# Second attention of a transformer kernel: q's split stacked by DMA, reciprocals in pairs, new orders of work on every engine

## The chip, the cores and the metric

One core of a Trainium2 chip runs the whole program in one launch. The metric is the device time in microseconds (us) of one execution. Three runs of the kernel before gave 1553.55, 1548.76 and 1550.9 us, a median of 1550.9 us.

## The reference

The input is x, 1024 tokens of 256 features, in float32. Four blocks follow each other, each with a layer norm ahead of it and a residual around it:

```python
x = x + attn_a(layernorm(x), ...)   # 16 heads of 128, a window of 64 keys, low-rank additions
x = x + ffn(layernorm(x), ...)      # 16 experts (4 chosen a token) and a shared part
x = x + attn_b(layernorm(x), Wq, Wk, Wv, Wo)
x = x + ffn(layernorm(x), ...)
```

The change is in the third block, called b in the kernel:

```python
q, k, v = heads(x @ Wq, 32), heads(x @ Wk, 8), heads(x @ Wv, 8)   # heads of 64
q, k = apply_rope(q), apply_rope(k)            # t1*cos - t2*sin, t1*sin + t2*cos
k, v = repeat(k, 4), repeat(v, 4)              # 4 query heads share one key head
scores = where(causal, q @ k.T / sqrt(64), min)
out = (softmax(scores) @ v) @ Wo
```

## The kernel before, in words

Products are done to float32 accuracy from two parts of each operand: a high part (a rounded copy in the type fp32r, made by ScalarE, ACT) and a low part (value minus high part, made by VectorE, DVE). The program has five engine streams written by hand with semaphores: TensorE (PE), DVE, ACT, GpSimd (POOL) and SyncE (SP), which only issues DMAs.

**Groups, heads, tiles.** Block b goes over 8 groups (one key head each), each of 4 query heads, 32 heads in all. A head has 8 query tiles of 128 rows (`SCORE_TILES`, the order 7, 6, 5, 4, 0, 1, 2, 3); tile t has 128 (t+1) keys. Per tile: PE makes the scores (`scores`) in one of two pairs of PSUM banks; DVE takes the row maxima (`row_max_b`, L691); ACT takes the exponentials and their row sums (`exp_b`, L1096); DVE takes the reciprocal of the sum (`row_inv_b`, L698), one tile at a time; POOL multiplies (`p_norm_b`, L844). Then the probabilities are turned in 12 chunks: PE turns (`turn`, L1495) into one of two banks, ACT copies the high part (`pt_hi_b`, L1106), DVE makes the low part (`pt_lo_b`, L706), PE multiplies with v (`products`). Chunk s can be turned only when the low part of chunk s-2 is out of the bank. Two sums a head (`o_add`, L714) put the result in `ot`.

**Pieces.** While the heads of group g run, q and k of group g+1 are made in 6 pieces of 128 x 512: pieces 0 and 1 are k, 2 to 5 are q (two heads a piece, one in partitions 0 to 63, the other in 64 to 127). A piece goes: projection on PE into bank 7 (`proj`); copy by ACT (`raw_b`, L1067); times cosine by DVE (`cos_b`, L667, writes `ra`); four DMAs issued by SP that swap the halves from `raw` to `rb` (`swap`, L292); two POOL operations (`rot_b`, L829 and L833); high part by ACT (`high_b`); low part by DVE (`low_b`).

**The stack.** For the scores, the high and the low part of one q head stand one above the other in the 128 partitions of `qh`: head 0 of a pair has its high part in partitions 0 to 63 and its low part in 64 to 127, head 1 the other way round. So `high_b` writes a q piece with two copies of 64 rows (L1081, L1082) and `low_b` with two subtractions of 64 rows (L681, L683). A k piece takes one copy (L1077) and one subtraction (L677) of 128 rows.

**What sets the order.** Each engine executes its steps in the order of a table `DUE` (10000 units are one head), which `steps` sorts for each engine by itself. A step waits on semaphores, and what is behind it on its engine waits with it. `w_hi_b` and `w_lo_b` split the next group's weights. The start of the block is written out step by step (`FIRST_PIECES` gives the order of the first six pieces; `first_raw`, `first_cos`, `first_high`, `low_b`), with `head(-1, ...)` as the two partial heads before group 0.

## Time and profile before

| | before |
|---|---|
| median of 3 runs | 1550.9 us |
| the profiled execution | 1545.96 us |
| its span | 1544.1 us |
| PE busy | 1426.9 us (92%) |
| DVE busy | 1112.4 us (72%) |
| ACT busy | 856.4 us (55%) |
| POOL busy | 627.5 us (41%) |

The profile comes from one execution, 1.9 us longer than its span. "Busy" is time in which an engine executes at least one instruction; matmuls are pipelined, so that the start of one and the end of the one before overlap. Block b lies from about 620 to 1290 us of the span. A figure over the whole span is a mean of blocks with different limits, so the rows below are mostly of this block alone.

### The profile page before, as it was taken

How to read it: one execution, taken by the hardware profiler on the slowest of the kernel's cores; microseconds unless marked ns; L12 is line 12 of the kernel's file. 1: busy time of each engine (PE TensorE's matmuls, PEld its weight loads, DVE VectorE, ACT ScalarE, POOL GpSimd, SP SyncE). 2: the span in 40 equal slices, each digit the busy share in tenths (PEclk: the TensorE clock that was granted, in tenths of full speed). 3: DMA queues.
4: the chain of work that ended last, by engine and by line, in shares of the span. 5: the costliest groups of instructions: out<-in, count | busy, mean ns of one | idle time of the engine just before them, and what ended most of it. 6: DMA issues, size and time to landing. Idle time of an engine off the chain costs nothing.

```text
span 1544.1 us, 27763 instructions
## 1 busy us (share of the span) xinstructions
PE 1426.9 (92%) x8632; PEld 1197.3 (78%) x8632; DVE 1112.4 (72%) x2132; ACT 856.4 (55%) x1917; POOL 627.5 (41%) x540
## 2 busy tenths in 40 slices
PE   6999999999899999788988889789898989899998
PEld 4888888888788888667776777667777769688887
DVE  5666666657565556579999998899999977565555
ACT  1444444454343333477777777677777765433332
POOL 3555555530000001376868686668686620000000
PEclk8999999999999999999999999999999999999999
DMA  3000000001111112110101010101010001111110
GB/s 110 25 25 26 25 24 24 16 23 44 49 42 51 41 51 73 38 28 21 35 18 39 15 39 17 33 20 37 17 28 18 18 21 43 49 52 51 41 51 28
DMA packets 30138, 54.25 MB, mean 35 GB/s; under 512 B 6273, under 2 KB 13761, under 8 KB 29761
## 3 DMA queue, kind: packets, MB, share of 16 engines
q1 hardware_dynamic: 30016, 52.78, 11.7%
q8 instruction: 59, 0.97, 0.3%
q14 instruction: 63, 0.51, 0.1%
HBM read 39.13 MB, written 1.05 MB: 26 GB/s over the span
## 4 chain that ended last, share of the span: by engine, by line
PE 69%; DVE 14%; issue 9%; ACT 4%; POOL 1%; DVEq 0%; ACTq 0%; POOLq 0%
PE ps L1187 49%; PE ps L1388 8%; PE ps L1495 6%; PE ps L1333 5%; DVE pt_lo L706 3%; DVE nmb L691 2%; DVE qh L683 2%; PE ps L1275 2%; DVE qh L681 2%; ACT pt_hi L1106 1%; DVE rb L408 1%; ACT pb_low L1096 1%; DVE ot L714 1%; DVE h_lo L600 1%; DVE hf L594 1%
## 5 line engine op out<-in xcount | busy, mean ns | idle before, releaser
L706 DVE TENSOR_TENSOR pt_lo<-ps,pt_hi 128x512 fp32r<-128x512 f32 (+3 forms) x384 | 206.5, 549 | 36.3 <-ACT pt_hi L1106 34.0
L1187 PE MATMUL ps<-kh,qh 128*128 128x512 f32 (+3 forms) x768 | 194.5, 362 | 19.9 <-DVE qh L683 10.8
L1106 ACT CAST pt_hi<-ps 128x512 fp32r<-128x512 f32 (+3 forms) x384 | 176.0, 480 | 60.0 <-PE ps L1495 53.7
L691 DVE TENSOR_REDUCE nmb<-ps 128x1 f32<-128x1024 f32 (+7 forms) x256 | 191.0, 746 | 14.7 <-PE ps L1187 13.3
L1187 PEld LDWEIGHTS ps<-kh,qh 128*128 128x128 f32 x768 | 135.7, 192 | 48.8 <-ACT pb_low L1096 10.3
L1187 PE MATMUL ps<-xt_hi,wf_hi 128*128 128x512 f32 x400 | 160.7, 402 | 9.4 <-DVE wf_lo L522 9.4
L1187 PE MATMUL ps<-pt_hi,vst 128*128 128x512 f32 (+3 forms) x384 | 163.5, 426 | 0.0
L1187 PE MATMUL ps<-xt_hi,wf_lo 128*128 128x512 f32 x400 | 159.3, 398 | 0.0
L1187 PE MATMUL ps<-xt_lo,wf_hi 128*128 128x512 f32 x400 | 159.3, 398 | 0.0
L1032 ACT CAST h_hi<-hf 128x512 fp32r<-128x512 f32 x100 | 62.1, 621 | 137.8 <-DVE hf L594 137.8
L588 DVE TENSOR_TENSOR sg<-sg,cwu 128x512 f32<-128x512 f32 x88 | 62.2, 707 | 105.2 <-ACT sg L1026 105.1
L1187 PE MATMUL ps<-pt_lo,vst 128*128 128x512 f32 (+3 forms) x384 | 135.2, 352 | 0.0
L1026 ACT ACTIVATE sg<-ps 128x512 f32<-128x512 f32 x100 | 59.9, 599 | 133.2 <-PE ps L1187 133.2
L844 POOL TENSOR_TENSOR pb_odd<-pb_odd,rib 128x1024 f32<-128x1024 f32 (+1 forms) x64 | 106.7, 1674 | 51.3 <-DVE rib L698 50.7
L923 ACT ACTIVATE pa<-ps,nmax 128x192 f32<-128x192 f32 x128 | 53.1, 424 | 130.9 <-DVE nmax L442 130.9
L1388 PE MATMUL ps<-wf_hi,h_hi 128*128 128x256 f32 x400 | 113.4, 284 | 3.2 <-DVE h_lo L600 3.2
L1388 PE MATMUL ps<-wf_hi,h_lo 128*128 128x256 f32 x400 | 112.8, 282 | 0.0
L1388 PE MATMUL ps<-wf_lo,h_hi 128*128 128x256 f32 x400 | 112.7, 282 | 0.0
L799 POOL TENSOR_TENSOR pa<-pa,rinv 128x384 f32<-128x384 f32 x64 | 53.0, 828 | 134.4 <-DVE rinv L448 134.4
L1333 PE MATMUL ps<-wos,ot_hi 128*128 128x256 f32 x512 | 95.9, 289 | 3.6 <-DVE ot_lo L486 3.6
L600 DVE TENSOR_TENSOR h_lo<-hf,h_hi 128x512 fp32r<-128x512 f32 x100 | 68.9, 689 | 41.2 <-ACT h_hi L1032 39.3
L821 POOL TENSOR_TENSOR wb_lo<-wb,wb_hi 128x768 fp32r<-128x768 f32 x8 | 15.6, 1950 | 202.9 <-ACT wb_hi L1010 202.9
(169 smaller groups left out, 4082.7 us busy)
## 6 DMA issues: line engine op xcount, KB each, us to landing
wf<-in_wf SPq DMA_DIRECT2D x50, 384.0 KB, 3.0
rb<-raw SPq DMA_DIRECT2D x192, 64.0 KB, 2.0
wa<-in_wa SPq DMA_DIRECT2D x16, 384.0 KB, 3.0
wb<-in_wb SPq DMA_DIRECT2D x8, 384.0 KB, 3.0
wo<-in_wo_a SPq DMA_DIRECT2D x16, 128.0 KB, 2.0
wo<-in_wo_b SPq DMA_DIRECT2D x16, 128.0 KB, 2.0
lb<-in_lb SPq DMA_DIRECT2D x16, 72.0 KB, 3.0
x_res<-in_x SPq DMA_DIRECT2D x4, 256.0 KB, 3.6
```

The source lines that it names most:

```text
L588: v.tensor_tensor(sg[:, b, :], sg[:, b, :], cwu[:, HALF * half:HALF * half + HALF], ALU.mult).then_inc(sem(f"{s}_sgc"), 1)
L600: v.tensor_tensor(h_lo[:, b, :], hf[:, b, :], h_hi[:, b, :].bitcast(F32), ALU.subtract).then_inc(sem(f"{s}_h_lo"), 1)
L691: v.tensor_reduce(nmb[:, par, i:i + 1], ps[:, b:b + 2, :].rearrange("p b k -> p (b k)")[:, 0:P * (t + 1)], AX.X, ALU.max, negate=True).the ...
L706: v.tensor_tensor(pt_lo[:, s % 3, at], ps[:, 4 + s % 2, at], pt_hi[:, s % 3, at].bitcast(F32), ALU.subtract).then_inc(sem("b_pt_lo"), 1)
L844: g_.tensor_tensor(pb(par, t), pb(par, t), rib[:, par, i:i + 1].broadcast_to([P, P * (t + 1)]), ALU.mult).then_inc(sem("b_pn"), 1)
L1026: s_.activation(sg[:, b, :], ps[:, b, :], ACT.Silu).then_inc(sem(f"{s}_silu"), 1)
L1032: s_.copy(h_hi[:, b, :], hf[:, b, :]).then_inc(sem(f"{s}_h_hi"), 1)
L1106: s_.copy(pt_hi[:, s % 3, at], ps[:, 4 + s % 2, at]).then_inc(sem("b_pt_hi"), 1)
L1187: return t_.matmul(o, l, r, start=start, stop=stop)
L1333: ins = t_.matmul(o, (ot_hi, ot_lo)[a][:, n % OT_RING, P * m:P * m + P], wos[:, h, w, :], start=h == 0 and k == 0 and m % 2 == 0, stop=h = ...
L1388: ins = t_.matmul(o, (h_hi, h_lo)[a][:, b, P * m:P * m + P], (wf_hi, wf_lo)[w][:, slot, 2 * D:3 * D], start=first and n == 0 and m % 2 == ...
L1495: last = t_.transpose(ps[:, 4 + s % 2, P * m:P * m + P], pb(par, base + m)[:, P * block:P * block + P], idf[:, :])
```

## The change

Four edits, all in block b.

1. `high_b` of a q piece is one copy of 128 rows from `ra` to the new tile `qt_hi`, `low_b` one subtraction of 128 rows into the new tile `qt_lo`. SP then issues four DMAs of 64 rows x 2 KB a piece (`stack`) that put the quarters where `qh` wants them. `scores` waits for the DMAs of the pieces that it reads; `raw_b` waits for the DMAs of the q piece two before (same half), since `qt_hi` and `qt_lo` have one slot a half. On SP, `stack` stands behind swaps, the load of the next weights, and ahead of the swaps of later pieces.
2. `row_inv_b` runs for odd i only, on two columns.
3. The table `DUE` has new values for all steps of b; scores of tile 0 are now issued nearly a head earlier, the low part of chunks 7 to 11 and the sums `o_add` come later in DVE's order. `proj` computes the head whose `o_add` it waits for.
4. At the start, DVE and ACT do the parts of pieces 4 and 5 ahead of head(-1, 1, 3), where the first row maxima and exponentials now are; ACT's `first_raw` of pieces 3 and 5 waits for the stack DMAs of pieces 2 and 3; the split of group 1's weights comes ahead of the first head.

```diff
@@ SP
+            def stack(n, piece, r):
+                pair, at = piece // 2 - 1, slice(HALF * (piece % 2), HALF * (piece % 2) + HALF)
+                sp.wait_ge(sem("b_lo"), n + 1)
+                for part, src, dst, which in ((qt_hi, 0, 0, 0), (qt_lo, 0, 64, 0), (qt_lo, 64, 0, 1), (qt_hi, 64, 64, 1)):
+                    sp.dma_start(qh[dst:dst + 64, pair, which, at].bitcast(F32),
+                                 part[src:src + 64, r, :].bitcast(F32)).then_inc(
+                        sem(f"b_stacked{piece}"), 16)
             def group(g, gp):
-                if not (isinstance(g, int) and g >= NG - 2):
-                    load_group(g + 2)
                 if not (isinstance(g, int) and g == NG - 1):
-                    for piece in range(6):
-                        swap(6 * (g + 1) + piece, piece % 2)
+                    n = 6 * (g + 1)
+                    for piece in range(4):
+                        swap(n + piece, piece % 2)
+                    stack(n + 2, 2, 0)
+                    stack(n + 3, 3, 1)
+                    if not (isinstance(g, int) and g >= NG - 2):
+                        load_group(g + 2)
+                    swap(n + 4, 0)
+                    swap(n + 5, 1)
+                    stack(n + 4, 4, 0)
+                    stack(n + 5, 5, 1)
             load_group(1)
-            for n in range(6):
-                swap(n, n % 2)
+            swap(0, 0)
+            swap(1, 1)
+            swap(2, 0)
+            stack(1, 2, 1)
+            swap(3, 1)
+            swap(4, 0)
+            stack(3, 3, 1)
+            swap(5, 1)
+            sp.wait_ge(sem("b_vout"), NT)
+            stack(4, 4, 0)
+            stack(5, 5, 1)
@@ DVE
-                    v.tensor_tensor(qh[64:128, pair, 0, at], ra[0:64, r, :],
-                                    qh[0:64, pair, 0, at].bitcast(F32), ALU.subtract)
-                    ins = v.tensor_tensor(qh[0:64, pair, 1, at], ra[64:128, r, :],
-                                          qh[64:128, pair, 1, at].bitcast(F32), ALU.subtract)
+                    ins = v.tensor_tensor(qt_lo[:, r, :], ra[:, r, :], qt_hi[:, r, :].bitcast(F32), ALU.subtract)
-                v.reciprocal(rib[:, par, i:i + 1], rsb[:, par, i:i + 1]).then_inc(sem("b_inv"), 1)
+                v.reciprocal(rib[:, par, i - 1:i + 1], rsb[:, par, i - 1:i + 1]).then_inc(sem("b_inv"), 2)
             head(-1, 1, QPG - 2)
-            head(-1, 1, QPG - 1)
             low_b(4, 0, FIRST_PIECES[4], 0)
             low_b(5, 0, FIRST_PIECES[5], 1)
+            head(-1, 1, QPG - 1)
@@ ACT
+                if isinstance(n, int) and n < 6:
+                    if n in (3, 5):
+                        act.wait_ge(sem(f"b_stacked{FIRST_PIECES[n - 2]}"), 64)
+                else:
+                    earlier = (piece - 2) % 6
+                    if earlier >= 2:
+                        act.wait_ge(sem(f"b_stacked{earlier}"), 64 * (g + 1) if piece >= 4 else 64 * g)
-                    s_.copy(qh[0:64, pair, 0, at], ra[0:64, r, :])
-                    ins = s_.copy(qh[64:128, pair, 1, at], ra[64:128, r, :])
+                    ins = s_.copy(qt_hi[:, r, :], ra[:, r, :])
@@ PE
                     pe.wait_ge(sem("b_lo"), 6 * g + (4 if hh < 2 else 6))
+                    for piece in (2, 3) if hh < 2 else (4, 5):
+                        pe.wait_ge(sem(f"b_stacked{piece}"), 64 * (g + 1))
-                        after(pe, "b_ot", 2 * (QPG * g + hh))
+                        after(pe, "b_ot", 2 * (QPG * g + heads_before(hh, i)))
@@ DUE (three of the 17 rows)
-    "inv": [-7333, -5571, -3963, -1688, -1674, -694, 44, 2103],
+    "inv": [-3513, -3512, 158, 159, 2001, 2002, 4819, 4820],
-    "pt_lo": [673, 2143, 2647, 2921, 5181, 6125, 6452, 7556, 8136, 9242, 9746, 9869],
+    "pt_lo": [3651, 4305, 5646, 5967, 6740, 6802, 7803, 10136, 10431, 11671, 12899, 13375],
-    "low": [13396, 17882, 27446, 29557, 44833, 47488],
+    "low": [17629, 24257, 26441, 28306, 45983, 46970],
```

Per group, where k pieces are 0 and 1 and ^ marks a piece that belongs to the group before in the table, ACT's new order in the first head of a group is exp 0, chunk 3, high 4^, exp 1, chunks 4 and 5, high 5^, exp 2, chunk 6, raw 0, exp 3, chunks 7 and 8, exp 4, raw 1; DVE's is max 0, chunk 1, (reciprocal), chunk 2, max 1, chunk 3, low 4^, max 2, reciprocal, chunks 4 and 5, low 5^, max 3, chunk 6, cos 0, max 4.

## Rows read from the trace of the kernel before

**Rows 1.** The page, part 4: the chain that ended last, shares of the span.
```profile
PE 69%; DVE 14%; issue 9%; ACT 4%; POOL 1%; DVEq 0%; ACTq 0%; POOLq 0%
```
**Rows 2.** Windows: us, each engine's busy us (instructions), PEclk, DMA share, GB/s.
```profile
839.52:856.43 16.91, 15.87 (x104) 12.87 (x102) 15.99 (x36) 14.16 (x35) 13.38 (x13) 1.00 0.07 17
856.43:875.85 19.42, 15.58 (x97) 12.23 (x96) 18.64 (x37) 14.63 (x35) 12.39 (x10) 1.00 0.06 14
875.85:893.63 17.78, 17.32 (x110) 14.16 (x109) 14.55 (x32) 15.26 (x35) 12.84 (x11) 1.00 0.13 31
893.63:915.60 21.97, 18.80 (x104) 14.78 (x103) 21.38 (x38) 15.82 (x37) 17.98 (x13) 0.92 0.16 43
839.52:915.60 76.08, 67.57 (x407) 54.04 (x405) 70.57 (x139) 59.88 (x140) 56.59 (x47) 0.98 0.11 27
671.25:1235.05 563.80, 500.08 (x3005) 401.29 (x3004) 516.69 (x1013) 441.94 (x1023) 413.46 (x338) 0.97 0.10 26
```
**Rows 3.** Waits of 839.52 to 915.60: engine, line, for whom, total us, times, longest.
```profile
PE ps L1495 <- DVE pt_lo L706: 6.5, 7, 2.6
ACT pt_hi L1106 <- PE ps L1495: 6.4, 8, 2.1
DVE pt_lo L706 <- ACT pt_hi L1106: 3.6, 7, 1.9
```
**Rows 4.** Groups by line and form, DVE, 839.52 to 915.60: count, busy us, mean ns.
```profile
L683 DVE TENSOR_TENSOR qh<-ra,qh 64x512 fp32r<-64x512 f32 x4 | 6.1, 1524 | 0.1
L698 DVE RECIPROCAL rib<-rsb 128x1 f32<-128x1 f32 x33 | 4.6, 150 | 0.1
L681 DVE TENSOR_TENSOR qh<-ra,qh 64x512 fp32r<-64x512 f32 x4 | 5.4, 1358 | 0.1
L677 DVE TENSOR_TENSOR kh<-ra,kh 128x512 fp32r<-128x512 f32 x2 | 2.3, 1130 | 0.0
```
**Rows 5.** Timeline of DVE: start us, us, line, operation.
```profile
898.55 0.15 DVE L698 RECIPROCAL rib<-rsb 128x1 f32<-128x1 f32 x1
898.62 0.67 DVE L706 TENSOR_TENSOR pt_lo<-ps,pt_hi 128x512 fp32r<-128x512 f32 x1
900.26 2.18 DVE L681 TENSOR_TENSOR qh<-ra,qh 64x512 fp32r<-64x512 f32 x1
902.45 2.08 DVE L683 TENSOR_TENSOR qh<-ra,qh 64x512 fp32r<-64x512 f32 x1
904.56 0.69 DVE L706 TENSOR_TENSOR pt_lo<-ps,pt_hi 128x512 fp32r<-128x512 f32 x1
```
**Rows 6.** Timelines of POOL and PE in the same stretch; the last bracket is idle time before.
```profile
900.00 3.98 POOL L844 TENSOR_TENSOR pb_odd<-pb_odd,rib 128x1024 f32<-128x1024 f32 x2
905.30 0.44 PE L1495 MATMUL ps<-idf,z 128*128 128x128 f32 x2 [2.60 <-DVE pt_lo L706]
```
**Rows 7.** Instructions on tiles qh and raw: duration ns min/median/max, first and last start.
```profile
L1081 ACT CAST qh<-ra x32: 606/622/633, 634.7 to 1208.0; 64x512 fp32r<-64x512 f32 x32
L681 DVE TENSOR_TENSOR qh<-ra,qh x32: 684/1078/2268, 642.3 to 1212.9; 64x512 fp32r<-64x512 f32 x32
L292 SPq DMA_DIRECT2D rb<-raw x192: 507/591/781, 625.2 to 1196.3; - x192
DMA to landing us min/median/max: 1.9/2.0/3.1
```
**Rows 8.** Timelines of the block's start, 640 to 672 us: ACT, DVE, PE, POOL.
```profile
643.47 0.59 ACT L1067 COPY raw<-ps 128x512 f32<-128x512 f32 x1 [1.97 <-PE ps L1187]
642.25 0.68 DVE L681 TENSOR_TENSOR qh<-ra,qh 64x512 fp32r<-64x512 f32 x1
653.85 1.17 PE L1187 MATMUL ps<-kh,qh 128*128 128x512 f32 x4 [2.02 <-DVE qh L683]
661.63 3.54 POOL L844 TENSOR_TENSOR z<-z,rib 128x1024 f32<-128x1024 f32 x2
671.25 1.20 DVE L691 TENSOR_REDUCE nmb<-ps 128x1 f32<-128x1024 f32 x1
```

More of the change, by code:

```diff
@@ L89, in build @@
         ra = sb("ra", [P, 2, HALF])
+        own = ExitStack()
+        with own:
+            qt_hi = sb("qt_hi", [P, 2, HALF], F32R, own)
         rb = sb("rb", [P, 2, HALF])
@@ L156, in build @@
             vb = ot[:, 0, :, :].rearrange("p (g k) (t d) -> p g k t d", k=2, d=DB)[:, :, 1, :, :]
+            over = ExitStack()
+            with over:
+                qt_lo = sb("qt_lo", [P, 2, HALF], F32R, over)
             raw = sb("raw", [P, 2, HALF], c=own)
@@ L674, in low_b @@
                 r = half if r is None else r
-                at = slice(HALF * half, HALF * half + HALF)
                 if piece < 2:
+                    at = slice(HALF * half, HALF * half + HALF)
                     ins = v.tensor_tensor(kh[:, kp, 1, at], ra[:, r, :], kh[:, kp, 0, at].bitcast(F32),
@@ L722, in head @@
                         row_max_b(h, (hh + dh) % 2, i)
-                    elif kind == "inv":
+                    elif kind == "inv" and i % 2:
                         row_inv_b(h, (hh + dh) % 2, i)
@@ L1124, in head @@
                     elif kind == "raw":
-                        raw_b(piece, i)
+                        raw_b(piece, g + 1 + dh, i)
+                        if i == 5 and not (isinstance(g, int) and g + 1 + dh >= NG - 1):
+                            w_hi_b(g + 2 + dh)
                     elif kind == "high":
@@ L1130, in head @@
                             v_hi_b(g + 1, 1 - gp)
-                        if (kind, i) == ("raw", 5) and not (isinstance(g, int) and g >= NG - 2):
-                            w_hi_b(g + 2)
             def group(g, gp):
@@ L1168, in _ @@
             v_hi_b(0, 0)
+            w_hi_b(1)
             head(-1, 1, QPG - 2)
-            head(-1, 1, QPG - 1)
             first_high(4)
             first_high(5)
-            w_hi_b(1)
+            head(-1, 1, QPG - 1)
             all_groups(act, group)
@@ L1648, in pieces_before, with heads_before @@
     return 6 * g + 6 + (0 if isinstance(g, int) and g == NG - 1 else done)
+def heads_before(hh, piece):
+    return hh + (DUE["proj"][piece] % 10000 - DUE["products"][11]) // 10000 + 1
 def chunk_columns(slot):
```

35 lines of the change are left out of this document (17 added, 18 removed).

## The prediction

> **What bounds the kernel now.** I read the page first: over the span PE holds 69% of the chain that ended last and DVE 14% [rows 1]. That mean is of little use for one block, so the windows of busy time come next. Between the first row maxima of two successive groups, 839.52 and 915.60 us, lie 76.08 us; DVE is busy for 70.57 of them (93%), PE for 67.57 (89%), ACT for 59.88, POOL for 56.59 [rows 2]. In this block DVE is the fuller engine, and PE is close behind. The four heads of the group take 16.91, 19.42, 17.78 and 21.97 us, and the length follows whichever of the two is fuller: in the two long ones DVE is busy for 18.64 and 21.38 us, in the third PE is, for 17.32 of 17.78 [rows 2]. The waits say how DVE's load reaches PE: the longest entry is PE's turning of a chunk that waits for the low part, 6.5 us a group, once for 2.6 us [rows 3]. Groups by line and form say what makes the long heads long: eight subtractions of 64 rows (L681, L683), 5.4 + 6.1 = 11.5 us a group, though their fastest takes 0.684 us [rows 4, 7]. They stand one behind the other in DVE's order: at 900.26 us two of them take 2.18 and 2.08 us, the low part behind them starts at 904.56, and PE, idle for 2.60 us, goes on at 905.30 [rows 5, 6]. So the thing to price is DVE's time a group, and then how soon PE takes over as the limit.
>
> **The split of q.** Per piece two subtractions of 64 rows (1.358 + 1.524 us) become one of 128 rows. The k pieces show one of that shape, 1.130 us on average [rows 4]. Saved: 4 x (2.882 - 1.130) = 7.0 us of DVE a group. Bounds for one new subtraction: from the 0.684 us of the fastest of 64 rows to the 2.268 us of the slowest [rows 7]; that makes the saving between 11.5 - 9.1 = 2.4 and 11.5 - 2.7 = 8.8 us. I take 1.130, since it is the same shape and sits in the same traffic. On ACT one copy of 0.622 us a piece goes [rows 7], 2.5 us a group of 59.88 busy: worth nothing by itself, as ACT has 16 us of idle time a group.
>
> The spread of these subtractions has a visible cause: POOL started two multiplications of 3.98 us together at 900.00, and the two subtractions beside them end at about 902.4 and 904.5 [rows 5, 6]. The Trainium skill (SBUF — State Buffer, section "SBUF: two separate sides") says that a DVE operation with two SBUF inputs and a GpSimd operation that reads SBUF take a shared port pair as an exclusive lock for the whole instruction. The trace agrees: each of the two took about one POOL operation (3.98/2 = 1.99 us). By that rule the gain is in the number of locks asked for, four a group instead of eight, and the new table could spend it by putting all four beside POOL's longest operations; this is the second rival below, priced from the rows.
>
> **The stack DMAs.** 4 DMAs a q piece, 16 a group, on SP, beside 24 swaps and one load. An issue takes SP 0.591 us [rows 7]: 41 x 0.59 = 24 us of 76, so the queue is not full. The path matters more: low part ready, 4 issues (2.4 us), landing 2.0 us (a swap of half the bytes; bounds 1.9 to 3.1) [rows 7]: 4.4 us from the subtraction to the first user. Users are the scores two heads on, and ACT's raw copy of the q or k piece two later. By the new order low 4^ is over before max 2, and raw 0, which waits for its stack, stands behind exp 2 and chunk 6, with PE's scores, chunks and six projection matmuls before it; I count about 7 us between the two, against 0.7 + 4.4. Raw 1 and low 5^ stand alike, some 5 us apart after the landing of the other stack. Raw 4 and 5 are half a head or more behind. The swaps of raw 0 and 1 are queued on SP behind both stacks, so raw 0's land about when POOL has done its fifth multiplication and wants them, to within half a microsecond. I price all of this at 0 in steady state (at most the first user's wait, the third rival).
>
> **Reciprocals.** 16 of 32 a group go. One is 0.150 us [rows 4], but the next operation begins 0.07 us after its start (898.55, 898.62) [rows 5]: between 1.1 and 2.4 us a group, 1.1 taken. Half the tiles are released to POOL one exponential later; POOL has 19 us of idle time a group, which hides it.
>
> **The new orders.** DVE's need falls to 70.57 - 7.0 - 1.1 = 62.5 us a group. PE's stays at 67.57, less what its own short waits and lowered clock have put into it (the last head shows a granted clock of 0.92 after its stalls, the other three 1.00) [rows 2]. So PE becomes the limit, and what is late next is PE's own queue. How near it can come to being full is shown by the third head: 17.32 of 17.78, 97% [rows 2]. With 66.5 us of work and 96 to 97% the group takes about 69 us: 7.1 us less. As far as dependencies go the orders leave that room: scores, maxima and exponentials of one bank pair go round in about 10 us a head, chunks in about 9, against 17. A gain of nothing from the orders beyond the removed DVE time would give 76.08 - 8.1 = 68.0 while DVE limits, so both ways meet near 68 to 69.
> How often: from 671.25 to 1235.05 us there are 30 heads in 563.8 us [rows 2], in which all 28 of the later q pieces fall, 7 groups' worth: 7 x 7.1 = 50 us less.
>
> **The start.** Here the change costs. ACT's raw copy of piece 3, at 643.47 before, now waits for the stack of piece 2: its low part is there at about 642.3, SP is busy with a swap until 643.3, issues until 645.7 and the last lands at about 647.5: 4 us later than before. Then the swap, POOL's two operations (2 x 1.3), high and low part of piece 3, and a second stack (4.4 us): first scores at about 660 instead of 653.85 [rows 8]. Raw 5 waits for that same stack, then swap, POOL, high and low of piece 5 (0.6 + 4.4 + 2.6 + 0.6 + 0.7 = 9 us), all of it now ahead of the first maximum: about 669. From there the first head takes its old way to the first multiplications on POOL (before: 661.63) and to the next head's first maximum at 671.25 [rows 8]. I get 681 for that one, with a chunk or two more done than before: +9 us, bounds +4 (only the first wait counts) and +13.
>
> **Sum.** 1545.96 - 50 + 9 = 1505 us for an execution like the profiled one. That one lies 4.9 us below the median of the runs shown, so a median of about 1509 us.
>
> **Rivals.** (1) PE loses nearly all its waits: 65.5 us a group, if the pipelining overlaps in its 67.57 shrink too. For: PE needs no operation more. Against: two chunk banks couple three engines. 7 x 10.6 = 74 less, + 9: about 1485. (2) The lock: the four new subtractions fall beside long multiplications and take 2.27 each. DVE saves 2.4 + 1.1 = 3.5, the group 3.5 to 4: 26 less, + 9: 1534. For: max and exp order of the next head puts them right behind the first reciprocal, when POOL starts its longest pieces. Against: k's subtractions stand alike and average 1.130. (3) The stack wait on ACT's raw copies: everything behind raw 0 and raw 1, exponentials and chunks, is held until the quarters land. It decides as soon as it adds 41/7 = 5.9 us a group; two waits of the full path, 8.8 us a group, give 7 x 8.8 = 62 on top of 1509: about 1571, slower. For: raw 0 has only some 2 us to spare by my count, and SP serves in order. Against: a piece's DMAs are issued by an SP that stands waiting for them. (4) The change does what it says but the saved time only turns into DVE idle time, PE's turns waiting for ACT instead [rows 3]: within 0.3% of before, 1551.
>
> **Numbers.** Forecast 0.54 (its own range 1496 to 1524), rival 1 0.20, rival 2 0.14, rival 3 0.07, rival 4 0.05. Faster by over 0.3% (about what a measurement of this kernel can tell from no change, 4.7 us): 0.54 + 0.20 + 0.13 = 0.87; within: 0.05; slower: 0.08. The range for 8 in 10 is 1480 to 1538: rival 1 and 2 in it, 3 and 4 out.
>
> **What would show it.** Right: first maxima of two groups about 69 us apart, DVE about 62 busy in them, PE over 95%; four subtractions a group at about 1.1 us; SP waiting for low parts and never the raw copies for DMAs, save at the start, where the first scores begin at about 660 us. Wrong: ACT raw copies with DMA as releaser in steady state; subtractions near 2.2 us; a group of 73 us or more with PE waiting for DVE or ACT; a start that costs nothing or 15 us.

## The result and the profile after

| | before | after |
|---|---|---|
| median of 4 runs | 1549.85 us | 1532.78 us (1532.64 to 1533.83) |
| the profiled execution, its span | 1545.96, 1544.1 us | 1533.83, 1532.0 us |
| DVE busy over the span | 1112.4 us | 1047.9 us |
| PE busy over the span | 1426.9 us | 1432.4 us |

The changed kernel is faster by 1.1%: ratio 0.9891, 95% interval 0.9872 to 0.991. The median fell by 17 us, where the forecast had 41; between the two profiled executions, from which all rows come, it is 12 us, since the one of before lies 3.9 us below its median and the one of after 1.1 us above. Windows of the kernel after, in the columns of [rows 2]: the same four heads, these four together, the 30 heads from the first maximum of head 1 to the last one (heads are counted from 0), and then head 0.

One correction to how the prediction names its rows: the stretch of [rows 2] does not lie between the first maxima of two groups. It runs from the first maximum of head 10 to that of head 14. It still holds one head of each place in the table, so it is as long as a group; "group" means this stretch below.

```profile
845.75:861.92 16.17, 16.06 (x100) 12.61 (x98) 14.58 (x30) 14.31 (x35) 14.54 (x13) 1.00 0.07 18
861.92:880.70 18.78, 16.43 (x98) 12.52 (x98) 15.73 (x31) 13.84 (x34) 12.29 (x10) 1.00 0.38 93
880.70:898.95 18.25, 17.69 (x107) 13.90 (x105) 14.62 (x29) 14.81 (x36) 13.50 (x12) 1.00 0.12 31
898.95:917.66 18.71, 17.42 (x104) 13.60 (x104) 16.74 (x30) 14.40 (x35) 15.89 (x13) 1.00 0.37 85
845.75:917.66 71.91, 67.60 (x406) 52.63 (x404) 61.67 (x117) 57.35 (x136) 56.22 (x47) 1.00 0.24 58
684.90:1223.89 538.99, 502.40 (x3017) 393.37 (x3015) 456.40 (x865) 425.78 (x997) 408.81 (x337) 0.99 0.23 54
669.40:684.90 15.50, 11.02 (x37) 8.15 (x38) 6.96 (x14) 7.77 (x19) 8.84 (x7) 0.50 0.15 35
```

The group is 71.91 us long, not 76.08, and DVE is busy for 61.67 us of it (forecast 62.5). PE holds 67.60 of 71.91 us, 94%; the forecast had it over 95% of 69. The 30 heads take 538.99 us instead of 563.80 [rows 2]: 24.8 us less, forecast 50. (Seven times the 4.2 us of this group would be 29; 2.6 us of the difference are in one stretch of four heads, described at the end, which takes 78.9 us after and 80.5 before.) The first maximum of head 1 comes at 684.90 instead of 671.25 [rows 2]: 13.65 us later, forecast 9. What follows the last maximum is 0.95 us shorter. Together -24.8 + 13.65 - 0.95 = -12.1 us, which is the difference of the two profiled executions.

Waits of the kernel after, first in the group (845.75 to 917.66), then over the 30 heads:

```profile
POOL pb_low L871 <- DVE rib L725: 7.8, 4, 3.8
POOL rb L856 <- DMA rb<-raw: 4.6, 2, 2.6
PE ps L1530 <- DVE pt_lo L733: 2.4, 3, 1.4
ACT raw L1101 <- DMA qh<-qt_hi: 2.1, 2, 1.1
ACT qt_hi L1115 <- POOL ra L860: 1.7, 1, 1.7
...
ACT raw L1101 <- DMA qh<-qt_hi: 13.9, 12, 2.0
ACT qt_hi L1115 <- POOL ra L860: 11.8, 7, 1.7
PE ps L1530 <- DVE pt_lo L733: 17.9, 23, 2.2
```

PE's turning waits for the low part 2.4 us a group, where it was 6.5 [rows 3]. The cover that the forecast gave the stack does not quite hold: ACT's raw copy waits for the stack DMAs twice a group, 1 us each.

POOL's waits for a swap, 4.6 us a group, are something else. The two of this group end at 868.26 and 887.12 us, and the raw copies ahead of them had waited for PE, not for the stack. The same wait in before, in e16 (the new order without any stack) and in e1 (the stack, but raw copies that never wait for it), both described below:

```profile
863.72 0.59 ACT L1101 COPY raw<-ps 128x512 f32<-128x512 f32 x1 [1.47 <-PE ps L1220]
882.61 0.59 ACT L1101 COPY raw<-ps 128x512 f32<-128x512 f32 x1 [0.89 <-PE ps L1220]
...
POOL rb L829 <- DMA rb<-raw: 0.5, 1, 0.5
POOL rb L834 <- DMA rb<-raw: 4.5, 2, 2.5
POOL rb L865 <- DMA rb<-raw: 4.5, 2, 2.6
```

So it came with the new order, which puts the rotation close behind the raw copy: over the 30 heads it is 4.0 us before and 33.2 after.

Groups by line and form in the same stretch, and the instructions on the new tile over the whole span (columns as in [rows 4] and [rows 7]):

```profile
L711 DVE TENSOR_TENSOR qt_lo<-ra,qt_hi 128x512 fp32r<-128x512 f32 x4 | 4.5, 1122 | 0.0
L725 DVE RECIPROCAL rib<-rsb 128x2 f32<-128x2 f32 x16 | 2.5, 154 | 0.0
...
L711 DVE TENSOR_TENSOR qt_lo<-ra,qt_hi x32: 679/1102/1552, 641.2 to 1199.8; 128x512 fp32r<-128x512 f32 x32
L306 SPq DMA_DIRECT2D qh<-qt_lo x64: 592/597/607, 643.6 to 1202.6; - x64
DMA to landing us min/median/max: 2.3/2.3/2.7
```

Four subtractions take 4.5 us a group, 1.122 us each. Before, eight took 11.5 [rows 4]: 7.0 us less, the term of the forecast to the tenth. Over the 30 heads DVE is busy for 456.4 us instead of 516.7, which is 8.0 us for every four heads (forecast 8.1). So the missing time is not on DVE.

Of the start, ACT's raw copies and parts and then DVE's part of piece 5 with the first two maxima behind it (start us, us, line, operation, idle before):

```profile
647.34 0.59 ACT L1101 COPY raw<-ps 128x512 f32<-128x512 f32 x1 [6.83 <-DMA qh<-qt_hi]
660.54 0.59 ACT L1101 COPY raw<-ps 128x512 f32<-128x512 f32 x1 [4.41 <-DMA qh<-qt_hi]
667.74 0.62 ACT L1115 CAST qt_hi<-ra 128x512 fp32r<-128x512 f32 x1 [4.84 <-POOL ra L860]
...
668.39 1.09 DVE L711 TENSOR_TENSOR qt_lo<-ra,qt_hi 128x512 fp32r<-128x512 f32 x1 [4.77 <-ACT qt_hi L1115]
669.40 2.21 DVE L718 TENSOR_REDUCE nmb<-ps 128x1 f32<-128x1024 f32 x2
```

### The profile page after: what moved, and what is told of

It reads as the page before. It is cut to its first block, busy times and chain, and to the rows that moved or that the text cites. A ratio compares the mean times of both kernels' runs of the same rounds, so it can differ in the third digit from the quotient of the medians.

```text
span 1532.0 us, 27754 instructions
## 1 busy us (share of the span) xinstructions
PE 1432.4 (93%) x8632; PEld 1191.2 (78%) x8632; DVE 1047.9 (68%) x1972; ACT 836.4 (55%) x1885; POOL 623.9 (41%) x540
## 4 chain that ended last, share of the span: by engine, by line
PE 58%; issue 15%; POOL 15%; DVE 7%; ACT 2%; POOLq 0%; DMA 0%; SPq 0%; DVEq 0%; ACTq 0%
PE ps L1220 39%; PE ps L1421 8%; PE ps L1366 6%; POOL pb_odd L871 4%; POOL yt L871 3%; POOL rb L856 2%; PE ps L1530 2%; POOL z L871 2%; PE ps L1308 2%; POOL pb_low L871 2%; POOL ra L860 1%; DVE pt_lo L733 1%; DVE rb L439 1%; DVE nmb L718 1%; DVE h_lo L631 1%
## 5 line engine op out<-in xcount | busy, mean ns | idle before, releaser
L1220 PE MATMUL ps<-kh,qh 128*128 128x512 f32 (+3 forms) x768 | 204.0, 376 | 20.8 <-DMA qh<-qt_hi 9.0
L1220 PEld LDWEIGHTS ps<-kh,qh 128*128 128x128 f32 x768 | 132.3, 196 | 43.9 <-issue 12.8
L1220 PE MATMUL ps<-pt_hi,vst 128*128 128x512 f32 (+3 forms) x384 | 155.9, 406 | 2.9 <-DVE ra L698 2.9
```

Of the source, the lines that this page charges most:

```text
L1220: return t_.matmul(o, l, r, start=start, stop=stop)
```

## The experiments

All ratios are to the kernel before, timed beside each kernel on the same chip (its median was 1549.85 us beside after and 1546.6 to 1548.8 us beside the others); 4 runs of each kernel. "Head 1" is its first maximum, "group" the time from the first maximum of head 10 to that of head 14, "30 heads" as above; these three come from the profiled execution. That execution lies within 1.9 us of the median in all kernels but three: before (3.9 us below), e16 (6.0 above) and e13 (5.0 above). Four kernels serve for timing alone: e5 and e6 leave work out, and in e8 and e16 the q parts come out in the wrong rows.

| kernel | median us | ratio (95%) | head 1 | group | 30 heads |
|---|---|---|---|---|---|
| before | 1549.85 | 1 | 671.25 | 76.1 | 563.8 |
| after | 1532.78 | 0.9891 (0.9872-0.991) | 684.90 | 71.9 | 539.0 |
| e8 before, one subtraction | 1497.80 | 0.9666 (0.965-0.9682) | 668.76 | 69.4 | 519.2 |
| e16 the same in the new order | 1528.37 | 0.9878 (0.9862-0.9895) | 678.89 | 74.6 | 546.8 |
| e2 new order, old split | 1582.43 | 1.0219 (1.0202-1.0236) | 680.74 | 78.3 | 592.5 |
| e3 stack in the old order | 1675.07 | 1.0829 (1.0806-1.0851) | 676.68 | 91.0 | 685.4 |
| e12 e3, own memory | 1596.16 | 1.0311 (1.0287-1.0334) | 673.41 | 84.3 | 611.3 |
| e15 second subtraction on POOL | 1597.05 | 1.0322 (1.0305-1.0339) | 671.27 | 85.3 | 616.2 |
| e1 after, own memory | 1522.40 | 0.9837 (0.9821-0.9853) | 680.22 | 71.1 | 531.6 |
| e4 e1, swap 5 earlier | 1521.70 | 0.9826 (0.9809-0.9842) | 679.48 | 71.1 | 533.0 |
| e5 e1, less PE | 1520.75 | 0.9823 (0.9806-0.9839) | 680.39 | 70.2 | 530.1 |
| e6 e1, less POOL | 1504.58 | 0.9713 (0.9697-0.973) | 678.90 | 68.9 | 516.9 |
| e9 e1, high 3 later | 1524.02 | 0.9838 (0.9821-0.9855) | 680.57 | 71.2 | 534.5 |
| e10 e1, rotation 4 later | 1520.82 | 0.9826 (0.9802-0.9851) | 680.76 | 71.0 | 530.8 |
| e11 e1, single reciprocals | 1522.55 | 0.9838 (0.9816-0.986) | 678.06 | 70.8 | 534.3 |
| e13 e10 and e11 | 1521.90 | 0.9828 (0.9806-0.9849) | 679.92 | 72.0 | 537.4 |
| e14 e1, pieces by twos | 1518.99 | 0.9818 (0.9801-0.9834) | 680.11 | 71.1 | 530.9 |
| e17 e14, first maximum first | 1516.42 | 0.9796 (0.977-0.9821) | 676.01 | 70.9 | 529.2 |

### Was DVE's saving sized right?

**e8_before_one_low.** The kernel before, with one subtraction of 128 rows and no stack; ACT still copies twice. The parts of q come out in the wrong rows, but every engine's work has the size that the forecast priced.

```diff
-                    ins = s_.copy(qh[64:128, pair, 1, at], ra[64:128, r, :])
+                    ins = s_.copy(qh[:, pair, 1, at], ra[:, r, :])
-                    v.tensor_tensor(qh[64:128, pair, 0, at], ra[0:64, r, :], ...)
-                    ins = v.tensor_tensor(qh[0:64, pair, 1, at], ra[64:128, r, :], ...)
+                    ins = v.tensor_tensor(qh[:, pair, 0, at], ra[:, r, :],
+                                          qh[:, pair, 1, at].bitcast(F32), ALU.subtract)
```

> The kernel before with one subtraction of 128 rows a q piece in place of two of 64 (ACT's second copy on 128 rows; the split of q comes out in the wrong rows); no stack DMAs, old table, old start. It takes the prediction's DVE saving alone, 7 us a group, without the path it was bought with. Theory (the old order, freed of 7 us of DVE in its long heads, gains nearly all of it): group 69 to 70 us, 1500 to 1508 us, faster than the changed kernel. Rival (PE becomes the limit near 72 us in any order): group 72 us, 1520 us.

Measured: 1497.80 us, 50.7 us less than before. Its group, and its subtractions in it:

```profile
823.19:892.59 69.40, 65.38 (x406) 52.64 (x405) 64.51 (x134) 59.21 (x140) 56.62 (x47) 1.00 0.12 30
...
L681 DVE TENSOR_TENSOR qh<-ra,qh 128x512 fp32r<-128x512 f32 x4 | 6.3, 1570 | 0.0
```

The group is 69.40 us, the 69 of the forecast, and PE is busy for 94% of it. Here a subtraction takes 1.570 us, more than after's 1.122, and DVE's busy time falls by 6.1 us only; the group falls by 6.7. Over the 30 heads 44.6 us are gained (forecast 50), and 2.5 us more ahead of them. So what the forecast said holds in the old order: DVE was its limit, its time comes out of the group at least one for one, and then 69 us is reached. What is missing in the changed kernel lies in what it does besides.

Why does the same subtraction take 1.122 us on average in one order and 1.570 in another? It depends on what POOL does when it starts. DVE and POOL in after:

```profile
901.71 1.84 POOL L848 TENSOR_TENSOR wb_lo<-wb,wb_hi 128x768 fp32r<-128x768 f32 x1
902.95 1.16 DVE L711 TENSOR_TENSOR qt_lo<-ra,qt_hi 128x512 fp32r<-128x512 f32 x1
...
868.10 0.68 DVE L711 TENSOR_TENSOR qt_lo<-ra,qt_hi 128x512 fp32r<-128x512 f32 x1
868.26 1.66 POOL L856 TENSOR_TENSOR rb<-rb,rope 128x512 f32<-128x512 f32 x1 [1.95 <-DMA rb<-raw]
```

In the first pair POOL is at work already and ends at 903.55; the subtraction ends 0.56 us later by these rounded figures. In the second POOL starts after the subtraction, which takes 0.68 us. All 128 q subtractions of before, after and e8 follow this: the 99 that started while a POOL operation was running ended 0.54 to 0.55 us after it, and the other 29 took 0.68 to 0.69 us.

### What the stack and the new order cost

**e2_old_split.** After, with before's copies and subtractions; the stack's DMAs and all waits for them go. This is the new order alone (with the paired reciprocals and the new start).

```diff
-                    ins = s_.copy(qt_hi[:, r, :], ra[:, r, :])
+                    s_.copy(qh[0:64, pair, 0, at], ra[0:64, r, :])
+                    ins = s_.copy(qh[64:128, pair, 1, at], ra[64:128, r, :])
-                    ins = v.tensor_tensor(qt_lo[:, r, :], ra[:, r, :], qt_hi[:, r, :].bitcast(F32), ALU.subtract)
+                    v.tensor_tensor(qh[64:128, pair, 0, at], ra[0:64, r, :], ...)
+                    ins = v.tensor_tensor(qh[0:64, pair, 1, at], ra[64:128, r, :], ...)
```

> The changed kernel with the old split of q (two copies and two subtractions of 64 rows, no stack DMAs); the new table, paired reciprocals and the new start order stay. Theory (the time comes from DVE's removed subtractions): DVE busy 68 to 69 us a group, group 75 us or more, first maximum at about 663 us, 1550 to 1556 us, slower than the changed kernel by 1 to 1.5%. Rival (the gain is the new order's own): group about 73 us, 1535 us or less.

**e3_old_order.** After, with all 17 rows of before's table, and at the start with the parts of pieces 4 and 5 behind head(-1, 1, QPG - 1) again, on DVE and ACT: the stack alone. Two of the rows:

```diff
-    "inv": [-3513, -3512, 158, 159, 2001, 2002, 4819, 4820],
+    "inv": [-7333, -5571, -3963, -1688, -1674, -694, 44, 2103],
-    "low": [17629, 24257, 26441, 28306, 45983, 46970],
+    "low": [13396, 17882, 27446, 29557, 44833, 47488],
```

> The changed kernel with the old table DUE and the old place of the parts of pieces 4 and 5; stack DMAs and paired reciprocals stay. Theory (the new table is needed for the stack: in the old one raw 0 and the scores of tile 0 stand too close behind the low parts): PE and ACT wait for stack DMAs 4 to 8 us a group, group 73 to 76 us, 1538 to 1550 us. Rival (only DVE's time counts): group about 70 us, 1520 us.

Windows of the same group in e2 and e3, and e3's waits in it:

```profile
855.98:934.32 78.34, 70.31 (x406) 54.98 (x404) 68.67 (x122) 60.46 (x140) 56.30 (x47) 0.96 0.10 26
```
```profile
887.42:978.41 90.99, 70.94 (x404) 56.55 (x404) 61.73 (x116) 57.57 (x134) 54.32 (x47) 0.92 0.19 46
```
```profile
DVE pt_lo L733 <- ACT pt_hi L1139: 19.1, 15, 5.3
POOL pb_odd L871 <- DVE rib L725: 14.9, 2, 11.1
ACT raw L1101 <- DMA qh<-qt_hi: 7.7, 2, 5.7
```

In the old order the stack takes away far more than it gives: 91.0 us a group, where 73 to 76 were expected, with ACT held up to 5.7 us for the DMAs (rival 3's mechanism) and POOL up to 11.1 us for reciprocals. I put the second down to pairs in a table row that had been made for single ones; no run in the old order changes that alone. In the new order the old split takes 78.3 us, 2.2 more than in its own order although DVE has 1.9 us less to do (68.67 against 70.57 [rows 2]). This group shows less than the whole: over the 30 heads it is 592.5 against 563.8, 28.7 us more, and head 1 comes 9.5 us later. So the new order is not free: by itself it is worse.

**e16_new_order_one_low.** e8's split in after's table, start and reciprocals (e2, with these two lines):

```diff
+                    ins = s_.copy(qh[:, pair, 1, at], ra[:, r, :])
+                    ins = v.tensor_tensor(qh[:, pair, 0, at], ra[:, r, :], qh[:, pair, 1, at].bitcast(F32), ...)
```

> The new table, paired reciprocals and new start with one subtraction of 128 rows a q piece and no stack DMAs (the split of q comes out in the wrong rows): the counterpart of e8_before_one_low_b, which has the old table, old start and single reciprocals and took 1497.8 us with groups of 69.4 us. Theory (the new order itself, made for the stack's delay, is some 2 us a group slower, as with two subtractions: 78.3 against 76.1): group 71 to 72 us, first maximum at about 663 us, 1518 to 1522 us. Rival (the stack's waits make the difference, the order is as good as the old one): group 69 us, about 1506 us.

Measured 1528.37 us, with this group:

```profile
840.41:915.03 74.62, 69.80 (x406) 54.86 (x404) 62.74 (x117) 59.39 (x140) 55.92 (x47) 0.95 0.11 28
```

Against e8 no engine gets an operation more, and DVE is busy for less (62.74, 64.51), yet the group is 5.2 us longer (PE is busy for 69.80 us instead of 65.38, at a granted clock of 0.95 instead of 1.00). The cost of the order (with the pairs and the new start) is thereby measured without stack or raw waits: 30.6 us in all (1528.37 - 1497.80). In the profiles it is 10.1 us at the start (head 1 at 678.89 against 668.76) and 27.6 over the 30 heads; since the profiled execution of e16 lies 6.0 us above its median, some 22 of these 27.6 are left for a usual one, 3 us for every four heads (an estimate). The 5.2 us of this one group are more than that because of one head:

```profile
856.54:878.86 22.32, 18.78 (x98) 14.88 (x98) 17.19 (x31) 14.86 (x36) 11.94 (x10) 0.85 0.05 13
```

In it PE was idle twice for a low part, for 1.77 and 1.26 us, and its granted clock is 0.85. The same head takes 18.78 us in after, at 1.00; the other three differ by 0.7 us at most.

The three kernels e8, e16 and after make the sum. By their ratios to before, 0.9666, 0.9878 and 0.9891, the new order takes away 0.0212 of the time and the stack in it 0.0013, which is inside the intervals. Nearly the whole distance between the changed kernel and e8 is the order's.

**e12_old_order_own.** Is it only the raw copies' wait that spoils e3? e3, where the parts get memory of their own (as in e1, below), and with single reciprocals.

```diff
-                v.reciprocal(rib[:, par, i - 1:i + 1], rsb[:, par, i - 1:i + 1]).then_inc(sem("b_inv"), 2)
+                v.reciprocal(rib[:, par, i:i + 1], rsb[:, par, i:i + 1]).then_inc(sem("b_inv"), 1)
```

> e3_old_order (old table, old start) with the memory of its own for the q parts and single reciprocals: raw copies no longer wait for stacks. Theory (in the old order the stack hurts in two places, the raw copies and the first scores of each pair of heads): ACT's waits for stack DMAs are gone, PE's of about 6 us a group stay, group 76 to 80 us, 1560 to 1590 us. Rival (only the raw waits hurt): group 70 us, 1505 us, as in the kernel before with one subtraction. Second rival (only the first scores' wait hurts): group 85 or more, 1640 us or more.

Measured 84.3 us a group (76 to 80 expected), 1596.16 us: better than e3 and still slower than before. Two changes were made at once, so their shares in the gain stay open. What is left of the trouble, PE's and POOL's waits in the group and two entries of SP's queue:

```profile
PE ps L1228 <- DMA qh<-ot: 6.3, 2, 5.4
POOL rb L865 <- DMA rb<-raw: 7.5, 2, 7.1
...
922.57 6.48 SPq L312 DMA_DIRECT2D qh<-ot  x8
929.18 4.41 SPq L303 DMA_DIRECT2D rb<-raw  x7
```

The path from subtraction to scores, some 4.7 us (four issues of 0.6, landing in 2.3), does not fit into the old order even where nothing is overwritten: PE waits up to 5.4 us for it. And SP serves in order. The raw copy of the next piece had ended at 920.21 us, but its swap stands behind eight stack DMAs and is issued at 929.18, 9.0 us later; POOL waits up to 7.1 us for such a swap. The stack in the old order thus delays what has nothing to do with it.

**e15_low_on_pool.** Another way without DMAs: before, with the second subtraction of each q piece on POOL.

```diff
-                    ins = v.tensor_tensor(qh[0:64, pair, 1, at], ra[64:128, r, :], ...)
+                pool.wait_ge(sem("b_hi"), n + 1)
+                g_.tensor_tensor(qh[0:64, pair, 1, at], ra[64:128, half, :],
+                                 qh[64:128, pair, 1, at].bitcast(F32), ALU.subtract).then_inc(sem("b_lo2"), 1)
```

> The kernel before with the second of the two subtractions of a q piece on POOL, old table, old start, no stack (the first six pieces as before). It takes 4 x 1.5 = 6 us a group from DVE, which POOL has idle (19 us), and issues no DMA. Theory (any relief of DVE in the old order is worth its whole size, as the one subtraction's 6.7 us was): group 70 to 71 us, 1505 to 1515 us, faster than the changed kernel. Rival (POOL's waits for the high parts hold its multiplications and with them the turns): group 74 us or more, 1535 us or more.

Measured 1597.05 us, 85.3 us a group: the rival. DVE has 5 us less to do (65.40 busy), but users wait up to 6 us for POOL:

```profile
PEld ps L1207 <- POOL qh L858: 6.0, 1, 6.0
```

Four operations put in POOL's order at table values guessed by hand cost more than their length; this says nothing of a table made for them.

### The raw copies' wait

**e1_wait_on_high.** The parts lay over `raw` and `rb`. Here they lie in columns of `ot` that no one uses yet (for the last group one of them in `wb`), and ACT waits for the stack only where it writes the next high part.

```diff
@@ ACT, raw_b
-                    earlier = (piece - 2) % 6
-                    if earlier >= 2:
-                        act.wait_ge(sem(f"b_stacked{earlier}"), 64 * (g + 1) if piece >= 4 else 64 * g)
@@ ACT, high_b of a q piece
+                        earlier = piece - 2 if piece >= 4 else piece + 2
+                        act.wait_ge(sem(f"b_stacked{earlier}"), 64 * (g + 1) if piece >= 4 else 64 * g)
@@ memory
+            def qt_lo(r):
+                return ot[:, 1, NG * 2 - 2 + r, :].bitcast(F32R)
```

> The changed kernel, but the q parts have memory of their own (unused columns of ot, the last group's in wb), so that the raw copies need not wait for the stack DMAs; the copy into qt_hi waits for them instead. Theory (the start is long because raw 3 and raw 5 wait for stacks, and in steady state these waits, 13.9 us in all, are mostly hidden): first maximum at about 664 us instead of 669.4, group still 71 to 72 us, about 1525 us. Rival (the start is long because the parts of pieces 4 and 5 now stand ahead of the first maximum): first maximum at 668 or later, 1531 us. Second rival (the raw waits hold every group): group below 70 us, 1515 us or less.

Measured 1522.40 us, 10.4 less than after (8 by the ratios to before, whose intervals do not touch): head 1 4.7 us earlier, the 30 heads 7.4 us shorter. The raw copies' wait is a real but small part of what is missing.

**e4_swap_first.** e1, with the swap of piece 5 ahead of the second stack at the start.

```diff
-            stack(3, 3, 1, 0)
             swap(5, 1)
+            stack(3, 3, 1, 0)
```

> As e1_wait_on_high, and at the start SP issues the swap of piece 5 ahead of the stack of piece 3. Theory: the first maximum waits for raw 5, swap, POOL, high and low of piece 5; with the swap ahead it comes 3 to 4 us earlier than in e1_wait_on_high, at about 661 us, about 1521 us. Rival (PE's or POOL's chain after the first maximum sets the start): no difference from e1_wait_on_high.

Measured 1521.70 us, no difference. The first maximum comes 0.7 us earlier, where 3 were expected: SP's order is not what mainly holds piece 5.

### What limits the rest: PE, POOL or the couplings

**e5_less_pe.** e1 without the products of the low part with v.

```diff
                 mm(ps[:, bank, at], vst[:, gp, block, :], pt_hi[:, s % 3, at], block == 0, ...)
-                mm(ps[:, bank, at], vst[:, gp, block, :], pt_lo[:, s % 3, at], False, ...)
```

> e1_wait_on_high without the products of the probabilities' low part with v (about 9 us of PE a group left out; DVE, ACT and POOL do all they did). Theory (PE's queue is the limit of a group, as the prediction had it: PE 67.2 of 71.1 us busy): the group falls by 6 us or more, to 63 to 65 us, where DVE's 61.6 takes over; about 1475 us. Rival (the order couples the engines, and PE waits in turn for chunks, POOL and DVE whatever it has to do itself): the group falls by 3 us or less, 1500 us or more.

**e6_less_pool.** e1, where POOL multiplies 128 columns of each tile only.

```diff
-                g_.tensor_tensor(pb(par, t), pb(par, t), rib[...].broadcast_to([P, P * (t + 1)]), ...
+                g_.tensor_tensor(pb(par, t)[:, 0:P], pb(par, t)[:, 0:P], rib[...].broadcast_to([P, P]), ...
```

> e1_wait_on_high with POOL's multiplications on 128 columns a tile only, the rest of the normalization left out. Theory (PE is the limit; POOL has 14 us idle a group, but the piece chain through POOL holds high 3): the group falls by 1 to 2 us, to 69 to 70. Rival (POOL's normalized tiles gate the turns): the group falls by 4 us or more.

Windows of the group in e1, e5 and e6:

```profile
838.16:909.30 71.14, 67.24 (x406) 52.52 (x404) 61.55 (x117) 57.50 (x136) 56.99 (x48) 1.00 0.24 59
```
```profile
838.18:908.40 70.22, 62.56 (x358) 46.86 (x356) 61.58 (x118) 57.01 (x136) 56.66 (x48) 0.98 0.25 59
```
```profile
832.73:901.63 68.90, 66.92 (x406) 52.67 (x404) 60.02 (x118) 56.98 (x136) 31.75 (x47) 1.00 0.25 61
```

e5 takes 4.7 us of busy time from PE (9 were expected) and the group gives back 0.9; the whole run is the same. PE, busy for 94% of e1's group, is therefore not its limit, and my theory that PE had taken over falls. Before, DVE was busy for 93% and was the limit, as e8 showed: the share does not tell the two apart. e6 takes 25 us from POOL and the group gives back 2.2, between the two expectations; the whole run gives back 18 us. I read this as a round through several engines (reciprocal, multiplication, turning, high part, low part) that ends last and that shorter multiplications shorten. That is not shown: DVE's busy time falls by 1.5 us in the same group as well, and its share in the gain was not taken apart.

**e9, e10, e11, e13: one coupling at a time.** e1 with high 3 (and low 3 behind it) later, with the rotation of piece 4 later, with single reciprocals, and with the last two together. The three rows in this order:

```diff
-    "high": [10304, 11959, 20292, 22604, 40401, 41876],
+    "high": [10304, 11959, 20292, 24640, 40401, 41876],
-    "rotate": [3935, 7296, 14785, 20377, 30609, 34693],
+    "rotate": [3935, 7296, 14785, 20377, 33500, 34693],
-    "inv": [-3513, -3512, 158, 159, 2001, 2002, 4819, 4820],
+    "inv": [-4034, -3512, -499, 159, 1700, 2002, 3652, 4820],
```

> e1_wait_on_high with high 3 two steps later on ACT and low 3 one step later on DVE (the new table puts high 3 0.38 heads behind raw 3, and ACT waits 1.7 us a group for POOL there). Theory (this wait is passed on to a chunk and to PE): the long second head falls from 18.8 to about 17.5 us, the group to about 70 us, 1513 us. Rival (it is hidden, or the stack of piece 3 becomes late for the next group's first scores): no gain, 1521 to 1525 us.

> e1_wait_on_high with POOL's rotation of piece 4 behind the fourth multiplication of its head instead of ahead of the first. Theory (POOL is the chain: in two heads a group a rotation that waits 2 to 2.6 us for its swap DMA stands ahead of the four multiplications that the next head's first turn waits for): the head with piece 4 falls from 18.2 to about 16 us, the group from 71.1 to 69, about 1508 us. Rival (the heads are held by other couplings of the order, as leaving out 5 us of PE work a group changed nothing): group 70.5 or more, 1519 us or more.

> e1_wait_on_high with the reciprocals tile by tile again, each placed right behind its exponential in the new table. Theory (pairing lets POOL's first multiplication start one exponential later, 1 us on the loop from one head's first turn to the next): group 68 to 70 us, 1500 to 1514 us. Rival (DVE's 16 saved instructions are worth more, or POOL is not the loop): group 71 to 72, 1522 to 1530 us.

> e10_rotate4_later and e11_single_inv together. Theory (both are on POOL's chain): group 66 to 68 us, 1490 to 1500 us. Rival: no more than the better of the two alone.

None tells itself from e1 (1520.8 to 1524.0 us). In e10 the head that had waited for piece 4 falls from 18.2 to 17.5 us and the next one rises from 18.0 to 18.6: given back at once. POOL's waits for swaps fall from 36.5 us to 15.2 over the 30 heads and the time stays, so those waits by themselves are not the cost of the order. The paired reciprocals, priced at 1.1 us of DVE a group, are worth nothing that these runs can tell once DVE has 9 us of idle time. In e11 two effects cancel: with single ones head 0 takes 13.36 us instead of 15.50, and the 30 heads take 2.7 us more.

**e14_pieces_by_two.** e1, with the q pieces following each other in twos, as the two k pieces do; raw, cos, rotate and high move alike, and low 1 to 20500.

```diff
-    "proj": [2962, 5984, 12664, 20628, 30385, 32448],
+    "proj": [2962, 5984, 12962, 15984, 32962, 35984],
-    "low": [17629, 24257, 26441, 28306, 45983, 46970],
+    "low": [17629, 20500, 25983, 26970, 45983, 46970],
```

> e1_wait_on_high with the q pieces made by twos in the first, second and fourth head of a group, each pair placed in its head as the k pieces are (POOL's rotations behind the fifth multiplication, raw copies in the middle of the head), so that the stack of piece 3 is ready most of a head earlier. Theory (the single pieces at the head's start hold PE, ACT and POOL in turn, each too near its successor): group 68 to 70 us, 1500 to 1515 us. Rival (any such order ends near 71): 1520 us or more.

Measured 1518.99 us (1517.39 to 1520.6), against 1522.40 for e1 on another chip; their ratios' intervals overlap. The group is the same (71.12).

### The start

**e17_first_max_first.** e14, with the parts of pieces 4 and 5 out of the first maximum's way: on DVE behind head(-1, 1, QPG - 1), on ACT inside it, behind exponential 4.

```diff
+            head(-1, 1, QPG - 1)
             low_b(4, 0, 0, FIRST_PIECES[4], 0)
             low_b(5, 0, 0, FIRST_PIECES[5], 1)
-            head(-1, 1, QPG - 1)
@@ ACT, in head
+                    if isinstance(g, int) and (g, hh, kind, i) == (-1, QPG - 1, "exp", 4):
+                        first_high(4)
+                        first_high(5)
```

> Own place for the parts and pieces by twos (as in the kernel of 1519, whose first row maximum was at 664.70 us, POOL's first multiplication of head 0 at 670.14 and the first chunk's turning at 676.36), and besides: the parts of pieces 4 and 5 on ACT come behind exponential 4 of head 0 instead of ahead of exponential 0, those on DVE behind maximum 4. Theory A (the start pays for its order: the first maximum stands behind pieces 4 and 5, which the first head doesn't need): first maximum near 660, as soon as the first scores (658.2) are done, first maximum of head 1 some 3 to 4 us earlier, total 1514 to 1517, ratio about 0.979. Theory B (the first head is limited by PE at half its clock and by what comes behind maximum 4): first maximum near 660, but the parts only move behind it, head 1 begins at the same time as before, total 1518 to 1520.

Measured 1516.42 us (1515.82 to 1517.12), the fastest version that does all of the work: 16 us below after, 15 by the ratios. Windows of head 0 before and in e17 (that of after stands above: 669.40:684.90):

```profile
655.13:671.25 16.12, 10.02 (x43) 7.26 (x43) 9.75 (x19) 11.08 (x24) 12.38 (x10) 0.79 0.06 15
```
```profile
659.35:676.01 16.66, 11.35 (x42) 8.30 (x42) 8.72 (x15) 8.43 (x20) 12.60 (x10) 0.62 0.28 64
```

The first maximum is 5.4 us earlier than in e14 (659.35, 664.70) and head 1's 4.1 us (676.01, 680.11). Theory A holds for the start; of the whole run, the intervals of the two ratios overlap.

## Why the prediction was right in sign and wrong in size

- **The sum.** For an execution like the profiled one the forecast was 1505 us and 1533.83 came. Of the 28.8 us, 25.2 are in the 30 heads (50 - 24.8), 4.65 at the start, and 0.95 came back behind the last maximum. The first is two things: even the old order gives 44.6 and not 50 (e8), and the changed kernel stands 19.8 us behind e8 (539.0 - 519.2).
- **DVE's saving: right.** 4 x (2.882 - 1.130) = 7.0 us a group was forecast, 7.0 measured; rival 2's dear subtractions (2.27 us) did not come, the longest of 32 took 1.552. That the result, 1532.78, stands next to rival 2's 1534 is chance. The Trainium skill (SBUF — State Buffer, section "SBUF: two separate sides") says that of a DVE operation with two SBUF inputs and a GpSimd operation that reads SBUF the one that starts second is blocked until the first is over. The traces agree, as shown under e8: a subtraction that meets a running POOL operation ends 0.54 to 0.55 us after it. The prediction had read this as one whole POOL operation for each subtraction; what counts is the rest of the one that is running, and the order sets it. That the mean in after, 1.122 us, came so near the 1.130 of the k pieces was luck in part, as e8's 1.570 shows.
- **What it is worth: right in the old order.** e8 shows 69.4 us a group against the forecast's 69, and 44.6 us over the 30 heads against 50.
- **The new orders: the step that failed.** "As far as dependencies go the orders leave that room" priced them at nothing. They cost 30 to 35 us, with either split of q: e16 is 30.6 us slower than e8 (in the profiles 10.1 at the start and 27.6 in the 30 heads, in an execution 6.0 above its median), and e2 is 34.9 us slower than the kernel before timed beside it (9.5 at the start and 28.7 in the 30 heads). The stack added to the new order changes the ratio by 0.0013 only. I had counted round times of single loops (10 and 9 us against 17) and PE's share of one good head; no run singles out which coupling of the five engines makes the order slower.
- **The stack's path: right in length, wrong at zero.** Issue 0.6 us each and landing 2.3 us (forecast 2.0, bounds 1.9 to 3.1). Raw 0 was counted to have 2 us to spare and is 1 us late, so the count was 3 us off; each of two raw copies a group waits 1 us. Own memory takes that away and gives 8 to 10 us in all (e1). The rest of the path's price is indirect: it is what rules out the old order as it stands (e3 and e12), so a gain of DVE time was paid for with a worse order.
- **PE as the next limit: wrong.** Its share came near the forecast (94%, forecast over 95), but e5 shows that less PE work changes nothing. 94% busy was read as the bound; it was only near it. Rival 1, which hung on PE, fell with it.
- **The reciprocals:** a group's 33 of 0.150 us became 16 of 0.154. DVE saves 0.9 us a group (over the 30 heads it is busy for 462.9 us in e11 and 456.0 in e1), priced at 1.1, and the time shows nothing of it (e11).
- **The start: right up to the first maximum, then wrong.** First scores at 660.6 (forecast 660), first maximum at 669.40 (forecast 669). Of the 4.65 us too few, 0.4 is this, 0.75 a slip of the prediction (its 681 less 671.25 is 9.75, and it took 9 into the sum), and 3.5 one assumption, that head 0 would then take 12 us, "with a chunk or two more done than before". It took 15.50, nearly as before (16.12). Two runs tell on what it hangs: with shorter multiplications it takes 13.41 (e6), with single reciprocals 13.36 (e11), so it hangs on that chain, which the pairs made longer. The granted clock is no rival here: PE, idle for 9.0 us before its first scores and for 7.4 before 671.90, ran at 0.50 in this head in after (1.2 of 2.4 GHz) and at 0.61 in e1, and both took 15.50 us; before it was 0.79.
- **Where the start's 13.65 us come from.** The forecast gave its 9 mostly to the DMAs. The order alone makes head 1 9.5 us late (e2), the stack alone 5.4 (e3, 676.68), both together 13.65, of which the raw copies' wait is 4.7 (e1) and the parts ahead of the first maximum 4 (e17).

**What stays open.** e1 to e17 bring the group from 71.9 to 70.9, and POOL's relief to 68.9. Which couplings of the order hold the 1.5 us between 70.9 and e8's 69.4, no run singles out. The 2.7 us from e16's group to after's lie in one head, where e16's clock fell; why it fell there and not in after stays open. A table worked out for a stack with own memory was not tried. And e2 and e16 change table, pairs and start at once, so how the order's cost falls to the start and to the 30 heads is known from the profiles only.

## What to carry to other kernels

When an edit frees an engine but adds a latency (a DMA hop of some 5 us), price the order that this latency forces, not the freed engine alone: a run with the freed time and without the new hop (e8), and one with the new order alone (e2, e16), separate the two at once. An engine at 94% in a loop whose heads overlap is not proven to be its limit; taking 5 us of work from it is the test. Compare such runs over all heads and not in one group: here one group said 5.2 or 2.2 us for an order that costs nearly the same with either split. A DMA queue that serves in order also passes on its waits: a DMA that stands behind one whose data are late is late too (e12, 9.0 us). And a staging buffer laid over a live one turns a DMA wait into a wait of the compute engine that next writes there.

## What the hardware showed that I had not expected

- A 64-row copy of 128 KB within on-chip memory lands 2.3 us after its issue (2.3 to 2.7), hardly more than a swap of 64 KB (2.0 [rows 7]).
- How long a DVE subtraction with both inputs in SBUF takes is set here by the POOL operation beside it: in before, after and e8 the q subtraction ends 0.54 to 0.55 us after the POOL operation that was running when it started (99 of 99), and takes 0.68 to 0.69 us where none was (29 of 29).
- At one place in the block PE and DVE pause for 1.6 to 3.4 us that the profile puts down to "issue". It is where the steps of group 4 begin, that is, where the program's loop, which takes groups 2 and 3 in its first pass and 4 and 5 in its second, goes back to its start (DVE's table takes maxima a head ahead, so group 4 begins with the first maximum of head 17, at 974.16 us before). In before, the entry into the loop and the way out of it show no such pause. The four heads from head 14 on, which hold this place, took 80.5 us before (the four before them 76.1), 75.6 in e8 (69.4) and 78.9 in after (71.9). Such a line of the kernel after:

```profile
976.62 1.71 PE L1220 MATMUL ps<-kh,qh 128*128 128x512 f32 x4 [3.03 <-issue]
```
